# Row maxima of the second attention taken in pairs, GpSimd's additions given stages of their own, and a new stage order

## The reference, cut to what matters

```python
h = tok(x); h = concatenate([h, txt], axis=1)
h = h + L0_attn(layernorm(h))       # scores clamped to 8 levels, no softmax
h = h + L0_ffn(layernorm(h))        # router, top-k tokens attend, the others get a mix; GELU
h = h + L1_attn(layernorm(h))       # softmax(q k^T / 4) v, 12 heads of 16
h = h + L1_ffn(layernorm(h))        # shared expert + 2 of 3 routed experts, SiLU gates
```

## Time and profile before

| | us |
|---|---|
| median of 3 runs | 4869.73 (4862.02 to 4880.92) |
| the profiled execution, its own time | 4867.58 |
| its span, first to last instruction | 4865.9 |
| TensorE busy / VectorE / ScalarE / GpSimd | 4159.1 / 2695.0 / 1762.4 / 416.9 |
| mean granted TensorE clock | 0.853 of full speed |

### The profile page before, as it was taken

One profiled execution on the slowest core, in us unless ns is written; L12 is line 12 of the kernel. 1 busy time (PEld: TensorE's weight loads), 2 busy tenths in 40 slices (PEclk: granted clock), 3 DMA queues, 4 the chain that ended last, 5 costly groups with the idle time before them and its releaser, 6 DMA issues.

```text
span 4865.9 us, 70034 instructions
## 1 busy us (share of the span) xinstructions
PE 4159.1 (85%) x27744; PEld 3253.4 (67%) x27744; DVE 2695.0 (55%) x7217; ACT 1762.4 (36%) x2774; POOL 416.9 (9%) x523
## 2 busy tenths in 40 slices
PE   2778888889888888888888888898888888888888
PEld 1556667677666776666677666677667677666666
DVE  2446555555655555655555656555656555655443
ACT  1224333334333344333334333334333333433332
POOL 2100011000001000001000001010001010001000
PEclk8668888888888888879888889888888988888888
DMA  4111111101111101101101111101111101111000
GB/s 112 32 25 34 32 26 36 31 22 33 32 26 36 36 17 34 35 22 36 34 19 34 35 22 36 36 18 33 36 29 29 36 21 29 36 25 16 13 13 4
DMA packets 154045, 147.12 MB, mean 30 GB/s; under 512 B 64359, under 2 KB 132026, under 8 KB 153722
## 3 DMA queue, kind: packets, MB, share of 16 engines
q1 hardware_dynamic: 153722, 142.64, 13.7%
HBM read 87.28 MB, written 7.91 MB: 20 GB/s over the span
## 4 chain that ended last, share of the span: by engine, by line
PE 63%; DVE 18%; SPq 5%; ACT 4%; DMA 4%; issue 3%; POOL 3%; POOLq 0%; DVEq 0%; ACTq 0%
PE area_a L1023 12%; PE area_n L1031 11%; PE area_b L1023 8%; PE area_m L1031 7%; SPq L451 4%; PE area_n L1248 4%; DMA k1s<-scratch 3%; PE area_n L1055 3%; DVE mx L927 3%; PE area_m L1198 3%; ACT pT_both L655 2%; PE area_b L1046 2%; PE area_a L1106 2%; DVE xn L730 2%; DVE scratch L938 1%
## 5 line engine op out<-in xcount | busy, mean ns | idle before, releaser
L927 DVE TENSOR_REDUCE mx<-area_n 91x1 f32<-91x273 f32 x1152 | 465.2, 432 | 273.7 <-PE area_n L1248 259.1
L1248 PE MATMUL area_n<-k1s,q1s 96*91 96x273 bf16 x1152 | 352.8, 364 | 226.1 <-DVE mx L927 124.2
L1031 PE MATMUL area_n<-w_dn,hid 128*91 128x192 f32 x2304 | 493.9, 379 | 41.3 <-DVE mrow L932 33.5
L1031 PEld LDWEIGHTS area_n<-w_dn,hid 128*91 128x91 f32 x2304 | 425.9, 190 | 89.4 <-issue 55.1
L1023 PE MATMUL area_a<-xT,w_gu 96*128 96x273 f32 x1536 | 409.0, 409 | 66.5 <-DVE y L887 38.2
L1023 PE MATMUL area_b<-xT,w_gu 96*128 96x273 f32 x1536 | 435.8, 431 | 0.0
L1248 PEld LDWEIGHTS area_n<-k1s,q1s 96*91 96x91 bf16 x1152 | 147.6, 146 | 399.0 <-DVE mx L927 229.3
L1023 PEld LDWEIGHTS area_a<-xT,w_gu 96*128 96x128 f32 x1536 | 283.9, 193 | 149.4 <-DVE y L887 48.0
L1023 PEld LDWEIGHTS area_b<-xT,w_gu 96*128 96x128 f32 x1536 | 308.2, 206 | 70.7 <-issue 0.5
L600 ACT ACTIVATE pa<-area_a,scal 91x820 bf16<-91x820 f32 x192 | 180.3, 939 | 313.5 <-PE area_a L1106 278.8
L990 DVE SCALAR_TENSOR_TENSOR outb<-area_n,cwt,outb 91x192 f32<-91x192 f32 x288 | 102.0, 407 | 272.9 <-PE area_n L1031 272.9
(11 more groups left out here) (242 smaller groups left out, 7776.7 us busy)
## 6 DMA issues: line engine op xcount, KB each, us to landing
img<-in_x SPq DMA_DIRECT2D x192, 392.0 KB, 3.5
q1s<-scratch SPq DMA_DIRECT2D x192, 102.4 KB, 3.4
k1s<-scratch SPq DMA_DIRECT2D x192, 102.4 KB, 4.5
out<-outb SPq DMA_DIRECT2D x32, 204.8 KB
q0s<-scratch SPq DMA_DIRECT2D x128, 25.6 KB, 3.8
k0s<-scratch SPq DMA_DIRECT2D x128, 25.6 KB, 2.2
pooled<-pooled_dram SPq DMA_DIRECT2D x128, 9.2 KB
tokens<-in_txt SPq DMA_DIRECT2D x32, 57.8 KB
```

The source lines that it names most:

```text
L927: v.tensor_reduce(mx[:, k:k + 1], N[0:TC, k % 2, 0:T], AX.X, ALU.max)\
L1031: last = mm(by_token(x)[:, c, :], lhs(i, c), w_, start=(i == 0), stop=(i == len(w) - 1))
L1248: mm(N[0:TC, k % 2, 0:T], q1s[0:SROWS, hh, c * TC:(c + 1) * TC], k1s[0:SROWS, hh, :], start=True, stop=True).then_inc(full["N"], 1)
```

## The change

Three edits. The 36 maxima tasks become 18 stages of two: TensorE writes both banks of N, and one VectorE instruction reduces both (91x2 from 91x546); TensorE waits at each stage until the whole area is taken (`begin` in place of `begin_bank`). The additions of GpSimd at `n0n` and `n1s` become stages `r2` and `r3`, each of these and `r1` waits until TensorE has filled N for the last `mx` stage ahead of it (`await_last`); the one at `n3s` waits for VectorE's `xn2` of `n3n`. And `TURN` is written anew. Names that moved against others: `pool.0` to `pool.5`, `n1n`, `gt`, `cl.4` to `cl.7`, `r1`, `pv.1`, `pw.0`, `pw.2`, `pv.2`, `ey.6` to `ey.11`, `dy.3` and `pr0`, and all of `mx`.

```diff
--- before.py
+++ after.py
@@ -49,19 +49,18 @@
 
 
 TURN = """
-tok n4s n4n n4f cw n0s n1s n2n n0n qk1.0 qk1.1 v2 n0f qk0.0 qk0.1 pool.0 n2f ey.0 v1 ez.0 ey.1 mx.0 mx.1 mx.2 n1n mx.3
-gate ez.1 mx.4 k1 pool.1 mx.5 v0 a0.0 mx.6 mx.7 ey.2 cl.0 cl.1 ez.2 mx.8 mx.9 mx.10 rta a0.1 cl.2 dy.0 pk0 r1 cl.3
-a0.2 mx.11 mx.12 mx.13 mx.14 mx.15 pk1 ey.3 ez.3 mx.16 mx.17 mx.18 gt vs mx.19 mx.20 pv.0 mx.21 mx.22 s1.0 s1.1 mx.23
-mx.24 og.0 ey.4 ez.4 mx.25 ey.5 ez.5 t1.0 mx.26 mx.27 mx.28 t1.1 rtb mx.29 mx.30 cl.4 cl.5 a0.3 mx.31 c1 mx.32 mx.33
-mx.34 mx.35 ct mt dy.1 a2.0 wo a2.1 a2.2 a2.3 pool.2 pool.3 a2.4 a2.5 cl.6 cl.7 pw.0 os.0 a2.6 pv.1 og.1 a2.7 ob.0
-a2.8 pool.4 a2.9 pw.1 os.1 a2.10 a2.11 ob.1 mg n3s n3n ey.6 ey.7 ez.6 pw.2 os.2 ey.8 ez.7 pool.5 ez.8 n3f a0.4 cl.8
-cl.9 dy.2 f0.0 f0.1 ob.2 f0.2 ey.9 ez.9 pr1 a0.5 n5s n5n cl.10 cl.11 fd ey.10 pv.2 ey.11 og.2 ez.10 n5f ez.11 pr0 dy.3
-rtr
+n4s tok n4n n4f cw n0s n1s n2n n0n qk1.0 qk1.1 v2 n0f qk0.0 qk0.1 n2f ey.0 ez.0 n1n v1 ey.1 mx.0 mx.1 gate ez.1 mx.2
+r3 k1 v0 a0.0 mx.3 ey.2 cl.0 cl.1 pool.0 ez.2 mx.4 mx.5 rta a0.1 cl.2 dy.0 pk0 cl.3 a0.2 mx.6 mx.7 pk1 ey.3 ez.3 mx.8
+cl.4 cl.5 mx.9 vs mx.10 pv.0 og.0 mx.11 s1.0 s1.1 mx.12 pool.1 ey.4 ez.4 ey.5 ez.5 r1 t1.0 mx.13 mx.14 t1.1 rtb a0.3
+mx.15 cl.6 cl.7 c1 mx.16 r2 mx.17 ct mt gt dy.1 a2.0 wo a2.1 a2.2 pv.1 a2.3 a2.4 og.1 a2.5 pw.0 a2.6 pool.2 os.0 a2.7
+a2.8 ob.0 a2.9 pw.1 os.1 a2.10 a2.11 ob.1 mg n3s pw.2 n3n ey.6 ey.7 ez.6 os.2 ez.7 ey.8 n3f ez.8 a0.4 pool.3 cl.8 cl.9
+dy.2 pool.4 f0.0 f0.1 ob.2 pool.5 f0.2 ey.9 ez.9 pr1 n5s n5n a0.5 fd ey.10 ey.11 cl.10 cl.11 ez.10 pv.2 ez.11 n5f og.2
+dy.3 pr0 rtr
 """.split()
 
 OFFSET = {"pool": -1}
-OFFSET.update({x: 0 for x in "tok n0s n0n n0f qk0 v0 vs a0 cl pv og pr0".split()})
-OFFSET.update({x: 1 for x in ("n1s n1n n2n n2f gate k1 v1 rta rtb pk0 gt pk1 s1 t1 c1 ct wo mg n3s n3n n3f f0 fd".split())})
+OFFSET.update({x: 0 for x in "r2 tok n0s n0n n0f qk0 v0 vs a0 cl pv og pr0".split()})
+OFFSET.update({x: 1 for x in ("r3 n1s n1n n2n n2f gate k1 v1 rta rtb pk0 gt pk1 s1 t1 c1 ct wo mg n3s n3n n3f f0 fd".split())})
 OFFSET.update({x: 2 for x in "n4s n4n n4f r1 qk1 v2 mx mt a2 pw os ob pr1 n5s n5n n5f rtr".split()})
 OFFSET.update({x: 3 for x in "cw ey ez dy".split()})
 FIRST_TURN, LAST_TURN = -1, BATCH + 2
@@ -385,6 +384,12 @@
             def await_full(self, x, stage, k=0):
                 self.eng.wait_ge(full[x], self.at(x, stage, k) + 1)
 
+            def await_last(self, x, stage, name):
+
+                before = [s_ for s_ in self.stages[:self.stages.index(stage)] if s_.startswith(name)]
+                if before:
+                    self.await_full(x, before[-1])
+
             def await_taken(self, x, stage, k=0):
                 self.eng.wait_ge(taken[x], self.at(x, stage, k) + 2)
 
@@ -538,20 +543,25 @@
                 for stage in t.stages:
                     if stage == "n0s":
                         inv_std("A", stage, 1, 0)
-                    elif stage == "n0n":
-
+                    elif stage == "n1s":
+                        inv_std("B", stage, 2, 0, twice=True)
+                    elif stage == "r2":
+
+                        t.await_last("N", stage, "mx")
                         pool.wait_ge(xn_ready["A"], t.done(stage))
                         add_row(tokens0, tokens0, bproj0).then_inc(base0_ready, 1)
-                    elif stage == "n1s":
-                        inv_std("B", stage, 2, 0, twice=True)
+                    elif stage == "r3":
+                        t.await_last("N", stage, "mx")
                         add_row(hb0, h0, bf2).then_inc(hb0_ready, 1)
                     elif stage == "n3s":
                         inv_std("B", stage, 2, 1)
                         pool.wait_ge(hb0_ready, t.done(stage))
+                        pool.wait_ge(xn_ready["B"], t.image(stage) * 2 + 2)
                         g.tensor_tensor(hb0[:, :, :], hb0[:, :, :], hs[:, :, :], ALU.add).then_inc(res0_ready, 1)
                     elif stage == "n4s":
                         inv_std("C", stage, 2, 0)
                     elif stage == "r1":
+                        t.await_last("N", stage, "mx")
                         if "dy.0" in t.stages:
                             t.await_taken("N", "dy.0")
                         add_row(hb1, h1, bproj1).then_inc(hb1_ready, 1)
@@ -924,7 +934,7 @@
                         last.then_inc(taken["N"], 1)
                     elif name == "mx":
                         t.await_full("N", stage)
-                        v.tensor_reduce(mx[:, k:k + 1], N[0:TC, k % 2, 0:T], AX.X, ALU.max)\
+                        v.tensor_reduce(mx[:, 2 * k:2 * k + 2], N[0:TC, :, 0:T], AX.X, ALU.max)\
                             .then_inc(taken["N"], 1)
                     elif name == "mt":
                         t.await_full("N", stage)
@@ -1242,11 +1252,13 @@
                     elif name == "mx":
                         if k == 0:
                             pe.wait_ge(stack_in, n * STACK_DMAS + STACK_DMAS)
-                        t.begin_bank("N", stage, "mx")
-
-                        hh, c = divmod(k, NC_)
-                        mm(N[0:TC, k % 2, 0:T], q1s[0:SROWS, hh, c * TC:(c + 1) * TC], k1s[0:SROWS, hh, :],
-                           start=True, stop=True).then_inc(full["N"], 1)
+                        t.begin("N", stage)
+
+                        for i in range(2):
+                            hh, c = divmod(2 * k + i, NC_)
+                            last = mm(N[0:TC, i, 0:T], q1s[0:SROWS, hh, c * TC:(c + 1) * TC], k1s[0:SROWS, hh, :],
+                                      start=True, stop=True)
+                        last.then_inc(full["N"], 1)
                     elif name == "mt":
                         t.begin("N", stage)
                         for c in range(NC_):
```

## The result

The changed kernel takes 4847.83 us (median of 11 runs, 4836.55 to 4856.86), the kernel before 4869.73 (11 runs). The ratio is 0.9954, 95% interval 0.9942 to 0.9965: 0.46% faster, where 3% was forecast. The profiled execution took 4846.17 us, its span 4844.4, at a mean granted clock of 0.855 (before 0.853).

What follows compares the result with a forecast made beforehand. TensorE was taken as the bound, losing time to idling and a lower clock. From 4867.6 us, 69 for the additions, 38 for `pw.2` and 39 for `pr0` came off, pairs 0: 4722, forecast as 4720, range 4650 to 4790.

Steps and rivals of the forecast that it cites:

- The additions: Chain feeding the stacks at the turn's head: moving GpSimd's additions ends it 2.17 us sooner a turn, 69 us gained.
- The bound at `pool.1`: VectorE's image reduction beside `r1`'s addition behind `mx.12`: slowed by 0 to 1.09 us a turn; taken as 0.
- The third addition: GpSimd's addition beside `n3n`: it delays a triple whose transposes TensorE reaches late; moving it gives nothing of itself.
- (a): `pw.2` moves between `mg` and `ey.6`, where TensorE waits for VectorE's reading of area A: gain 38 us.
- (b): `pr0` moves between `dy.3` and `rtr`, covering VectorE's reading of N at the router: gain 38.7 us.
- The pairs: Maxima stretch: pairs idle TensorE 8.3 us a turn against 3.9, offset by saved latency; taken as 0, bounds -2 to +4.4.
- starts fewer: Maxima: 18 reductions and matmul starts fewer save latency that the counted waits leave out; at most 2 us a turn.
- a walk through the order: Stages from `mx.0` to `dy.1` laid end to end by profile rows: 0.5 us a turn below before.
- four more us at most: Extra idling where VectorE has an expert product or `pool.0` before a pair's reduction: `mx.5` 0.9, `mx.9` 0.5, `mx.10` 0.7, `mx.11` 0.2.
- Rival 2: Maxima: pairs give the gain back, +3 us a turn, 4818 us; 4887 if DMA engines bind the stacks too; chance 0.20.
- Rival 3: Maxima: strict ping-pong on N lowers the clock, costing up to 7.5 us a turn; 5050 us, chance 0.15.
- Rival 1: Behind the stack wait: the clock recovers from 0.50 to 1.00, 3.2 us a turn; 4620 us, down to 4510; chance 0.15.

Runs made afterwards that it cites:

- the best order: Maxima stages spread apart among other TensorE stages, as singles; with GpSimd's additions put back to their places before the change, it took 4705.54 us.
- singles in the spread order: Against the kernel before: additions and outside stages moved, single maxima in an order spreading their stages among others; 4545.55 us, ratio 0.9369, repeated at 4541.28, 0.9324.

## Why the prediction was wrong

- **The additions (-69 us): right.** Head -2.06 us a turn, 66 us; the cast (L915, now L925) at 0.443; the stacks' landing did not become the limit. The cast's 1.08 us was read from this line of the turn's timeline, which the rows don't show:

```profile
2410.28 1.53 DVE L915 CAST scratch<-pT_both 96x546 bf16<-96x546 f32 x1
```

  What I left out is that the clock behind the removed idling rises with it: the same edit alone gave 90 us, and 160 in the best order. The bound at `pool.1` (0 to 1.09 us) was not tested by the change, since they didn't meet. In the kernel with singles in the spread order they did: 25 of its image reductions ran beside an addition for over half a microsecond, and none is slow:

```profile
L755 DVE TENSOR_REDUCE part<-img x192: 1065/1073/1086, 47.5 to 4099.8; 112x14 f32<-112x896 f32 x192
```

  So 0 was the right end; that is what the prediction took from the Trainium skill (VectorE: DVE Perf Modes, the perf-mode tier table, and the port rule that it names beside it), and the trace agrees. What I missed is the scaling of `smx`, 1.0 us in 31 turns: `await_last` waits for TensorE's filling, which says nothing of where VectorE is. It lay almost off the path (0.9948 without it, 0.9954 with it).
- **The third addition: right for the kernel before, and as said.** Beside `n3n` it cost nothing until `pw.2` moved; with `pw.2` moved it would have cost 1.08 us a turn.
- **(a) `pw.2` (-38 us): right**, -1.53 us a turn in its stretch, less 0.22 in the one before: 42 us.
- **(b) `pr0` and `dy.3` (-39 us): wrong in size.** 0.48 us a turn, 15 us. I asked only whether `og.2` and `ez.11` were late and not who held area N: `n5f` now stands directly ahead of `dy.3` in it, and `dy.3` waits for ScalarE's copy, 24.5 us. In the old order `pr0` lay between them and hid it.
- **The pairs, and the order of the stretch around them (both taken at 0): this is the step that failed.** The stretch of the maxima grew by 2.96 us a turn, 95 us. The idling itself was forecast well: six adjacent pairs at 1.0 us (0.81 measured), 0.9 and 0.5 more at `mx.5` and `mx.9` (0.55 each), 0.7 and 0.2 at the next two (0.61 and 0.24), 8.3 us against the 7.4 of the wait list (219.3 + 17.8 over 32). It was then set to nothing against "starts fewer" and a walk through the order, of which the record has only the result, 0.5 us a turn below before. (That passage speaks of "four more us at most" and lists 2.3; its 8.3 holds the 2.3.) Those latencies saved 352.8 - 298.5 = 54 us of busy time against 105 us of idling added. I also took the two causes for one: the pairs cost 2.1 us a turn, and the new order in this stretch, with singles, another 2.2 against the additions alone; the additions gave 1.3 of it back through the clock.
- **Rival 2 came out**, by its first mechanism (+3 us a turn, 4818), and lies under the measured time by the 24 us of (b) and 7 us of `mt` to `mg`. It had a chance of 0.20. **Rival 3** had the right place, TensorE in ping-pong on N, but the clock did not fall overall (0.853 to 0.855); the 7.5 us a turn that it charges stand in the prediction without a working. **Rival 1** did not come with the change: from 1.1 to 7.5 us behind `mx.0` the mean granted clock was 0.51 before and 0.53 after (turns 4 to 29). With singles in the spread order it is 0.76 there, and 0.877 overall.

The chain is: 4867.6 - 66 - 42 - 15 + 95 = 4840, against 4846.2 of the profiled execution.

**Open:** why the clock is lower with the last three pairs split (0.860) than with all of them (0.870) and with none (0.877); by which stages it is lost I could not pin down. Open too is what part of the new order's 2.2 us in the stretch belongs to which stage.

## What to carry to other kernels

Where two engines pass an area to and fro, the right to be one bank ahead can be worth more than fewer and longer instructions, as it was here in all three orders: price a merged stage by the hand-over (write, latency, read, release), count how many follow each other, and look for what else stands behind the longer instruction in its queue. When a stage is moved, list for its new neighbour every reader that still holds the same area, not only the data that it needs. Try the parts of a tangled change apart: here one of three edits carried all the gain (1.8%), and with the moves outside the maxima it gave 3.7%, with better places for the maxima 6.3% to 6.8%.

## What the runs showed of the hardware

- Work removed ahead of TensorE can be worth more than its length: 2.0 us of waiting removed from a turn gave 2.8 us (ratio 0.9817, 90 us over 32 turns), the rest as a higher granted clock in the 50 us behind (0.79 against 0.76).
- GpSimd's addition of 91x576 fp32 (1.40 us) slowed a cast of 0.44 us to 1.53, a normalising instruction of 0.37 us to 1.46, a clamp of 0.36 us to 1.58 and a scaling of two elements from 0.17 to 1.17. How short the VectorE instruction is doesn't matter: what counts is when the addition ends. In the traces of before and after the scaling ended 0.02 to 0.03 us behind the addition in all 31 cases, the normalising 0.12 us in all 32, the cast 0.30 to 0.31 us in all 30.
- Not slowed were reductions out of PSUM (62 of the changed kernel's lay beside an addition for more than half their length, 0.723 us at most), the one of 1.07 us out of SBUF (25 in the singles' spread order, 1.075 at most), and in the changed kernel a reciprocal of 91x3 (31 times, 0.172 us beside it and 0.171 without).
- Four kernels whose span times granted clock agreed within about 0.1% (3983 to 3988 us) had spans from 4544.8 to 4631.0 us, 1.9% apart. Of these 86 us TensorE was busy for 67 and idle for 19, with the same number of matmuls.
